# A gated delta-rule scan whose state is updated one leaf earlier, with one carry matmul for keys and queries

## What is computed

```python
def step(St, inp):
    kt, qt, vt, at, bt = inp
    Sk = jnp.einsum('bhij,bhj->bhi', St, kt)
    err = Sk - vt
    Sn = at[..., None] * St - (bt[..., None] * err)[..., None] * kt[:, :, None, :]
    ot = jnp.einsum('bhij,bhj->bhi', Sn, qt)
    return (Sn, ot)
```

## Time and profile before

| | |
|---|---|
| median of 3 runs | 8708.34 us (8691.14 to 8710.81) |
| the profiled execution's time | 8691.16 us |
| its span | 8689.2 us |
| scan phase in it | from about 1112 to 3980 us |
| projection phase in it | from about 194 to 1095 us |
| PE, DVE, ACT, POOL busy, whole span | 74%, 59%, 27%, 32% |

### The profile page before, as it was taken

How to read it: one execution, slowest core, us unless ns; L and a number is a source line. 1 busy time by engine, 2 the same in 40 slices (tenths; PEclk the granted TensorE clock), 3 DMA queues, 4 the chain that set the end, 5 groups by cost and what they waited for, 6 DMA issues and landing times. The chain is left out here.

```text
span 8689.2 us, 99856 instructions
## 1 busy us (share of the span) xinstructions
PE 6422.4 (74%) x25312; PEld 4362.9 (50%) x25312; DVE 5122.4 (59%) x8030; ACT 2321.9 (27%) x4571; POOL 2792.5 (32%) x4069
## 2 busy tenths in 40 slices
PE   2888746666666666667898987745528989898799
PEld 1766635555555555554456863322217832222587
DVE  3888846667676666765564221487887743433322
ACT  1222212222222222223342111244411233333111
POOL 0555557777777777772111111000000000000011
PEclk6999855555555555557998998856555578888899
DMA  4333343334343434332211013211103211111200
GB/s 163 120 136 136 131 103 89 94 82 97 84 97 84 95 82 98 84 84 83 69 47 54 22 51 122 65 29 36 30 1 68 51 39 30 39 29 33 94 29 27
DMA packets 939691, 631.50 MB, mean 73 GB/s; under 512 B 764768, under 2 KB 841056, under 8 KB 906080
## 3 DMA queue, kind: packets, MB, share of 16 engines
q1 hardware_dynamic: 939280, 627.52, 26.3%
HBM read 437.68 MB, written 192.81 MB: 73 GB/s over the span
## 5 line engine op out<-in xcount | busy, mean ns | idle before, releaser
L897 POOL TENSOR_TENSOR ffn_hid_low<-ffn_hid,ffn_hid_high 128x512 fp32r<-128x512 f32 x128 | 164.6, 1286 | 3560.3 <-ACT ffn_hid_high L887 3560.3
L298 PE MATMUL proj_acc<-proj_xn,proj_w 128*128 128x512 f32 x3072 | 732.5, 402 | 121.9 <-ACT proj_decay L344 87.8
L1413 POOL TENSOR_TENSOR scan_ud<-scan_ud,scan_ring 128x16 f32<-128x16 f32 (+6 forms) x1792 | 629.9, 352 | 548.0 <-DVE scan_ud L1516 412.5
L2150 PE MATMUL attend_ot<-attend_e,attend_v 128*64 128x512 f32 (+3 forms) x1280 | 678.0, 619 | 92.4 <-ACT attend_e L2177 92.4
L298 PEld LDWEIGHTS proj_acc<-proj_xn,proj_w 128*128 128x128 f32 x3072 | 598.3, 195 | 256.2 <-ACT proj_decay L344 90.8
L1442 POOL TENSOR_TENSOR scan_pq<-scan_qs,scan_ud 128x320 f32<-128x320 f32 (+3 forms) x512 | 655.8, 1307 | 0.0
L1516 DVE TENSOR_REDUCE scan_ud<-scan_pk 128x16 f32<-128x48 f32 (+6 forms) x1792 | 558.0, 311 | 67.2 <-DVE scan_pk L1513 6.7
L393 DVE SCALAR_TENSOR_TENSOR proj_y<-proj_raw,proj_cw,proj_y 128x2048 f32<-128x2048 f32 x144 | 575.6, 3997 | 19.1 <-DVE proj_y L389 2.9
L1774 PE MATMUL csum_sc<-csum_qk 96*128 96x512 f32 (+3 forms) x640 | 290.3, 570 | 395.6 <-ACT csum_e L1798 350.2
L1288 PE MATMUL scan_krow<-scan_kbd,scan_duT 128*128 128x64 f32 x1536 | 411.7, 432 | 166.5 <-ACT scan_duT L1200 166.5
L1320 PE MATMUL scan_zq<-scan_ring,scan_S 128*128 128x64 f32 x2048 | 453.3, 422 | 102.4 <-DVE scan_S L1562 102.4
(11 more groups left out here) (211 smaller groups left out, 13407.4 us busy)
## 6 DMA issues: line engine op xcount, KB each, us to landing
scan_abar<-decays SPq DMA_DIRECT2D x64, 1024.0 KB, 4.7
scan_kbd<-kbd SPq DMA_DIRECT2D x64, 768.0 KB, 4.4
csum_qk<-qk SPq DMA_DIRECT2D x96, 256.0 KB
cmax_qk<-qk SPq DMA_DIRECT2D x96, 256.0 KB
attend_qk<-qk SPq DMA_DIRECT2D x96, 256.0 KB
proj_beta_rows<-beta SPq DMA_DIRECT2D x16, 1024.0 KB, 8.1
stream_k<-proj_res SPq DMA_DIRECT2D x16, 1024.0 KB, 3.9
stream_beta_k<-proj_resb SPq DMA_DIRECT2D x16, 1024.0 KB, 3.9
```

Of the source, the lines that this page charges most:

```text
L298: mm = pe.matmul(acc[:, (j * TT + t) % 8, :], w[:, u, wh, j, k, :], xn[:, xh, k, t * TOK:(t + 1) * TOK], start=(p == 0 and k == 0), stop=( ...
L1413: pool.tensor_tensor(ud[:, l, t + 1, 1:t + 1, :], ud[:, l, t, 1:t + 1, :], a, ALU.mult).then_inc(dec_step, 1)
L2150: pe.matmul(ot[:, g % 2, lo:TOK], v[:, u, kt, :], e[:, x % RINGS, lo:TOK], start=(kt == 0), stop=(x == last_of[g])).then_inc(summed, 1)
```

## The change

The change has these parts:

- **State one leaf earlier.** The state of the next window now takes in the last leaf of the window before and leaves 0 to 2 of this one (`uw`, `kin` shifted by a leaf). `ds` and its additions to `S` are done during leaf 3, and the next `z` (`project`) follows. Leaf 3 reaches the next window through a fourth carry: a second Gram product per window (keys 8 tokens back, `gback`, `copy_back`) and a larger `kbd`.
- **One carry matmul.** `carry` multiplies a transposed leaf with keys' and queries' columns together (256 columns, result `y` in PSUM). Leaf 0 gets one too. VectorE takes `y` in at the start of each leaf, with two operations more.
- **Summed index innermost** in `pk` and `pq`, so that the sums read neighbouring elements, and the products read `ud` across.
- **Leaf decays as a sixth stream.** `project_phase` multiplies decays within each leaf of 8 tokens (`within`) and stores them; the scan loads them with the ring and drops `ge`. GpSimd's `tables` has 5 operations in place of 12.
- **Ring loads on ScalarE's queue** (`load_ring`), six DMAs in every second window. Gram numbers are made one window ahead, not two.

The core of the diff (shortened):

```diff
-            def carry_k(l, to, src, parity, first, last):
-                t = LEAF * (to - l - 1)
-                for b in range(2):
-                    mm = pe.matmul(krow[:, to % 2, 8 * b:8 * b + 8, 0, :], duT[:, src, :],
-                                   later(l, parity)[:, 0, 8 * b:8 * b + 8, t:t + LEAF], start=first, stop=last)
+            def carry(c, j, parity):
+                table = kbd[:, parity, KBD_AT[j]:KBD_AT[j + 1]].rearrange("p (w h t) -> p w h t", w=2, h=H)
+                t = LEAF * (c - j)
+                return pe.matmul(y, duT[:, TURNED[c] + j, :], table[:, :, :, t:t + LEAF], start=(j == 0), stop=(j == c))
...
+                    wait(pe, uw_copied, 2 * (w + 1))
...
+                    wait(pe, y_added, 4 * w + 4)
+                    wait(pe, yq_copied, 4 * w + 4)
+                    wait(pe, ut_copied, w + 1)
...
+                    wait(pe, qb_copied, 8 * (w + 1))
+                    wait(pe, s_added, 4 * (w + 1))
+                    project(n[0], n[1])
+                    broadcast_k(n[0], 0)
```

```diff
 # ScalarE, start of a window
+                copy_tr(w, 0, 0, 1)
+                copy_yq(w, 0)
+                copy_kin(w, tok)
+                if u == 0 and not first or u == WPC and not final:
+                    wait(act, kin_copied, w + 1)
+                    wait(act, table_step, 5 * (w + 1))
+                    load_ring(act, it if u == 0 else it + 1, 1 - u // WPC)
+                copy_slot(w, tok, 1)
+                if more:
+                    n = at(it, u, 1)
+                    copy_back(n[0])
+                    copy_gram(n[0])
```

```diff
 # VectorE, in a leaf, and the order of a window
+                yk = y[:, 0]
+                dve.tensor_tensor(ud[:, l, 1, 1, :], pk[:, l, 0, :, 0], yk[:, :, 0], ALU.add).then_inc(u_step, 1)
+                later = yk[:, :, 1:LEAF].rearrange("p h t -> p t h")
+                dve.tensor_tensor(later, later, ud[:, l, 1:LEAF, 0, :], ALU.mult).then_inc(y_scaled, 1)
+                wait(dve, y_scaled, 4 * w + l + 1)
+                dve.tensor_tensor(pk[:, l, 1:LEAF, :, 0], pk[:, l, 1:LEAF, :, 0], later, ALU.add).then_inc(y_added, 1)
...
+                    dve.tensor_reduce(ud[:, l, t + 1, t + 1, :], pk[:, l, t, :, 0:t + 1], AX.X, ALU.add).then_inc(u_step, 1)
+                    between(t)
...
+                leaf(w, 0, nothing)
+                if more:
+                    split_gram(at(it, u, 1)[0])
+                prepare_k(w, tok, parity, 1, LEAVES - 1, 2)
+                if not first:
+                    reduce_o(*before, 2)
                 prepare_q(w, parity)
-                leaf(w, 1)
-                leaf(w, 2)
+                leaf(w, 1, nothing)
+                if not first:
+                    reduce_o(*before, 3)
+                leaf(w, 2, nothing)
                 reduce_o(w, it, u, 0)
...
+                def add_state(t):
+                    if more and t >= LEAF - R:
+                        r = t - (LEAF - R)
...
+                leaf(w, 3, add_state)
                 reduce_o(w, it, u, 1)
```

More of the change, by code:

```diff
@@ L1149, in body @@
                         store_o(it - 1, 1)
[L1150 to L1151 removed]
+                if more:
                     load_rows(n[0], 2)
+                    load_rows(n[0], 3)
                     wait(sp, s_decayed, 4 * (w + 1))
                     load_abar(n[0])
[L1155 to L1170 removed]
+            run(sp, prologue, body)
             store_o(TURNS - 1, 1)
@@ L1273, in broadcast_q @@
                 wait(pe, rows_in[l], 64 * (w + 1))
+                first = rows_of(l, 1)
                 for b in range(2):
                     if l == 0:
-                        wait(pe, pre_step, 5 * (w + 1))
+                        wait(pe, pre_step, 6 * (w + 1))
                     else:
                         wait(pe, qb_copied, 8 * w + 2 * (l - 1) + b + 1)
-                    pe.matmul(zq[:, b, :], ones[32:34, :], rows[32:34, l, 512 * b:512 * b + 512],
+                    pe.matmul(zq[:, b, :], ones[first:first + 2, :], rows[first:first + 2, l // 2, 512 * b:512 * b + 512],
@@ L1292, in carry_q, with project @@
-            def carry_q(to, src, parity):
-                for l in range(to):
-                    t = LEAF * (to - l - 1)
-                    mm = pe.matmul(yq, duT[:, src + l, :], later(l, parity)[:, 1, :, t:t + LEAF], start=(l == 0), stop=(l == to - 1))
-                return mm
-            def turn_leaf(w, l, n):
-                wait(pe, u_step, 32 * w + 8 * (l + 1))
-                wait(pe, dec_step, 28 * w + 7 * (l + 1))
-                pe.transpose(tr[:, 0, :], ud[:, l, LEAF, 1:SLOTS, :].rearrange("p s h -> p (s h)"), idt[:, :]).then_inc(tr_done, 1)
-                wait(pe, tr_copied, 5 * w + n + 1)
+            def project(w, tok):
+                for h in range(H):
+                    mm = pe.matmul(z[:, h], S[:, h, :], ring[:, 0:2, h, tok:tok + WIN], start=True, stop=True)
+                mm.then_inc(z_done, 1)
@@ L1354, in body @@
-                wait(pe, yq_copied, 3 * w + 2)
+                wait(pe, y_added, 4 * w + 2)
+                wait(pe, yq_copied, 4 * w + 2)
+                turn_older(w, 2, 3)
+                for j in range(2):
+                    carry(2, j, parity)
+                turn_last(w, 2, 4)
+                carry(2, 2, parity).then_inc(y_done, 1)
+                broadcast_k(w, 3)
+                wait(pe, y_added, 4 * w + 3)
+                wait(pe, yq_copied, 4 * w + 3)
                 wait(pe, kin_copied, w + 1)
```

566 lines of the change are left out of this document (287 added, 279 removed).

## The result

The changed kernel takes 9155.1 us (median of 4 runs, 9148.97 to 9167.66), the kernel before took 8706.08 us beside it. The ratio is 1.0521, with a 95% interval of 1.0502 to 1.0539. The forecast was 9230 us, so its sign and mechanism were right and its size 75 us too high.

What follows compares the result with a forecast made beforehand. A chain of waits, not a full engine, was taken to bound the kernel. 8691 + 185 (longer windows) + 355 (ring loads) + 5 (prologue) = 9236 us, given as 9230; own range 9130 to 9350, wider 8940 to 9360.

Steps and rivals of the forecast that it cites:

- the last step of the sum: From 9236 us, against the profiled execution, to the forecast median of 9230; the median before was 17 us above that execution.
- Ring loads, +355: Six DMA issues on ScalarE ahead of the Gram copies delay leaf 1 by 11.8 us in 30 windows: +355 us.
- Rival 1: Ring DMA issues on ScalarE are short, 0.39 us each: +70 us in all, 8951 us; chance 17%.
- L0 to L1: Gap from leaf 0's start to leaf 1's, filled by VectorE's work: 9.3 us against 8.2, without the ring issues.
- L1 to L2: Gap from leaf 1 to leaf 2: later copies and wider carries make VectorE wait; 8.3 us against 6.6.
- L2 to L3: Gap from leaf 2 to leaf 3: broadcasts, transposes and three carries precede the last carry; 10.6 us against 8.3.
- Rival 2: The queue's additions hide: L1 to L2, L2 to L3 stay 6.6, 8.3; 8981 us (8%), or 8696 with short issues (3%).
- L3 to L0: Gap from leaf 3 to the next leaf 0, shortened by the earlier state update: 18.9 us against 21.1.
- z and the turn stand in one queue: On TensorE leaf 3's turn (0.84 us) stands behind z (7.08) and a key broadcast (0.75), losing most of the gain.
- faster sums don't help here: From leaf 1 to leaf 2 VectorE waits some 2 us anyway; output sums save 0.26 and 0.43 us each.
- Rival 3: TensorE's clock rises to 2.4 GHz: window 37.4 us, 8620 us in all; decides from 38.5 us a window; chance 5%.
- Rival 4: The tables come late under the ring's traffic, 5 us in each of 30 windows: 9390 us; chance 6%.

Runs made afterwards that it cites:

- ring_spread: Changed kernel with the six ring DMAs issued apart on ScalarE's queue: one, one, then four at the window's end; 8820.6 us, 1.0154 of the kernel before.
- turn_carry: Changed kernel with z in four groups, each behind its quarter of S, leaf 3's transpose before the last group and its carry right behind z; 8822.2 us.
- older_first: Changed kernel with the older leaves' transposes and carries ahead of the queries' second broadcasts on TensorE, ScalarE's copies in the same order; 9041.1 us.
- Quarters: Changed kernel with z's matmuls in four groups, each waiting only for its own quarter of the addition to S; 8896.9 us.
- sum_outer: Changed kernel with only the layout of the outputs' products put back, so that their sums read across memory again; 9194.4 us.
- all_spread: Changed kernel with the edits of ring_spread, turn_carry and older_first together; 8478.3 us, 0.9766 of the kernel before.
- all_early: all_spread with ring DMAs issued earlier, four of the six before the window's end; 8390.6 us, 0.9644 of the kernel before.
- ring_late: Changed kernel with all six ring DMAs issued on ScalarE after the window's last copy; 8864.8 us, 1.0182 of the kernel before.

## Why the prediction was right, point by point

- **Sign and mechanism.** Both added terms are where they were put: the window by itself, and the issues on ScalarE. By the sums of gaps, undoing only the place of the issues (ring_spread, -338 us) gives back the one; turn_carry (-316) and older_first (-111) more than give back the other. The total is nearer than its working by luck in one place, the last step of the sum, and further off by a term that the forecast had at nothing, the clock (both below).
- **Ring loads, +355:** measured +344, 11.5 us in 30 windows. Rival 1 has fallen: the waits are there, and a ring load is issued in 0.38 us only when none stands right ahead of it.
- **L0 to L1, L1 to L2, L2 to L3:** 9.3, 8.3 and 10.6 forecast, 9.03, 8.20 and 10.87 measured. VectorE's waits ahead of leaves 2, 3 and 0 were given as 2, 4.6 and 1.5 us and are 2.41, 3.85 and 2.22 in the window shown (means 2.4, 4.25 and 2.4). That the broadcasts ahead of the carries set L2 to L3 is shown by older_first. For L1 to L2 it explains 0.59 of 1.46 us; the rest (later `y`, carries of 256 columns) was argued, and no run took it apart. Rival 2 has fallen. The third gap is nearer to its forecast than its steps are: where the clock stays at 1.2 GHz it is 11.22 us, not 10.87.
- **L3 to L0, the term that was mis-sized:** 18.9 forecast, 17.60 measured; 1.3 us in 63 windows are 82 us, about the size of the whole error. The step was "the update matmuls end at 4.1 [...] four additions and three steps end at 9.0": the last addition ends at 2481.86, 7.7 us after leaf 3 (2474.18), and at 7.1 us in the window ahead of it, where the first addition starts 3.0 us after leaf 3. So the update was ready a good microsecond earlier than forecast in most windows, and additions and steps together took 4.1 us in place of 4.8. From the last addition to leaf 0 the forecast had 9.9 us; it is 10.4 (2481.86 to 2492.22). The early update is the clock's doing. In six of the 63 windows the clock stays at 0.50 from leaf 2 to the next leaf 0, and they come close to the forecast; one of them (window view, then VectorE), and last the first 3.0 us of the leaf 3 at 2428.86, whose clock is at 1.00:

```profile
2635.53:2653.86 18.33, 12.67 (x74) 10.40 (x73) 8.21 (x26) 1.35 (x4) 7.84 (x15) 0.50 0.17 59
...
2635.53 0.18 DVE L1550 TENSOR_TENSOR scan_ud<-scan_pk,scan_misc 128x16 f32<-128x16 f32 x1 [4.62 <-PE scan_misc L1329]
...
2639.45 0.69 DVE L1615 TENSOR_TENSOR scan_S<-scan_S,scan_misc 128x512 f32<-128x512 f32 x1 [1.28 <-PE scan_krow L1418]
...
2428.86:2431.86 3.00, 1.48 (x35) 1.07 (x33) 2.32 (x11) 1.07 (x3) 1.41 (x6) 1.00 0.10 6
```

The update is ready 3.9 us after leaf 3 there (4.1 forecast) and 3.0 where the clock is up; leaf 3 to leaf 0 is 18.3 us against 17.4, and leaf 2 to leaf 3 is 11.22 with VectorE's wait at the forecast 4.6. At 1.2 GHz throughout, the two gaps would thus be some 46 and 22 us longer over the scan (an estimate from 18.33 and 11.22 against the means).

- **The sum's last step** is wrong: 9236 us stood against the profiled execution, and with the 17 us up to the median it gives 9253, not 9230. Against 9253 the miss is 98 us, and the profiled execution (9148.97 us) is 87 below 9236; by the estimate above some 68 of these are the clock's.
- **"z and the turn stand in one queue":** shown. Quarters gave 4.06 us, the turn and carry 1.06 more.
- **Sums:** "faster sums don't help here" is shown by sum_outer. Taken at 1.7 ns per element, the product across was right: 339 ns against 0.15 + 112 x 0.0017 = 0.34 us.
- **Rival 3, the clock:** the kernel did not get faster, and the granted clock is 0.55 over the scan. But the clock does rise for a part of 57 of 63 windows, around leaf 3, which the forecast had at nothing; that is the mechanism of rival 3 in small. Its 38.5 us a window is the length at which the scan would make up for the loads ((38.5 - 44.2) x 63 = -359), and says nothing of when the clock rises.
- **Rival 4, late tables:** not seen. In windows with and without a load the median gaps from leaf 1 on are 8.20 and 8.20, 11.22 and 10.64, 17.41 and 17.41 us. The difference in the second pair goes with the clock: 11.2 to 11.4 us wherever it stays at 0.50 up to leaf 3, with a load or without.
- **Prologue and projection, +5 and 0:** the first leaf starts 1.2 us later than before, so both together cost about nothing; they were not measured apart.

## What to carry over

Removing work from a chain pays only as far as the in-order queues around it let it: here a detour got shorter by a leaf's length, and z behind four additions instead of two, two broadcasts ahead of the carries and six DMA issues ahead of a small copy cost more than that. Before moving a step, write down for each engine what stands behind it and who waits for that; the same arithmetic in another order went from 5.2% slower to 3.6% faster. The next wait can come from an engine that none of the edits touched, as GpSimd's did in leaf 3. Issue DMAs singly, into stretches where the issuing engine idles, and early enough to land.

## What the runs showed of the hardware

**The clock moves within a window.** In the kernel before it was 0.50 throughout the scan. In the changed one it is 0.87 in the stretch after leaf 3 starts, and 0.50 again at the end of the update matmuls:

```profile
2474.18:2477.00 2.82, 1.41 (x28) 1.20 (x30) 2.33 (x11) 1.07 (x3) 1.18 (x5) 0.87 0.45 99
...
2476.50:2477.00 0.50, 0.50 (x17) 0.50 (x16) 0.29 (x2) 0.00 (x0) 0.28 (x2) 0.50 0.70 279
```

Before the rise TensorE was busy 9.21 of 10.69 us with broadcasts and three wide carries; in the stretch at the high clock it was busy half of the time. The fall comes before the 4.2 us in which TensorE idles ahead of z. The clock has risen by the last carry into leaf 3 (0.70 us at 2473.35, in place of 1.22) and the transposes of `uw` behind it (0.60, where the keys' four take 1.06 in the earlier trace rows); this is why the update was ready early. In all_spread, three stretches behind leaf 3:

```profile
2534.44:2538.00 3.56, 2.12 (x37) 1.36 (x35) 1.61 (x8) 2.04 (x5) 3.13 (x5) 1.00 0.08 5
2538.00:2539.67 1.67, 0.00 (x0) 0.03 (x1) 1.52 (x6) 0.00 (x0) 1.02 (x3) 1.00 0.25 35
2541.00:2544.00 3.00, 3.00 (x16) 3.00 (x16) 2.96 (x7) 0.00 (x0) 2.48 (x6) 0.50 0.53 221
```

The clock is at 2.4 GHz while TensorE idles for 2.3 us ahead of z, and falls to 1.2 GHz when z, which starts at 2539.67 and runs without a pause, is about a microsecond old. So in both kernels the fall comes while TensorE is busy, and the work just before it is sparser than before the rise. Not every window shows a rise. One of all_early, which is as short as any here:

```profile
2461.92:2501.76 39.84, 34.25 (x182) 22.82 (x182) 26.88 (x87) 12.35 (x31) 30.27 (x51) 0.50 0.29 78
```

TensorE is busy 86% of it, and the clock stays at 1.2 GHz. What tells such a window from the others, and where the clock rises for good, was not found.

**An issue's length varies with other queues.** Six issues on ScalarE gave 2.30 us each from the fourth on in the changed kernel, but one each of 5.48 us (ring_late) and 5.67 us (ring_spread) at the window's end. In both cases SyncE had issued the load of `abar` 1 to 3 us before; ring_spread has:

```profile
2484.08 0.38 SPq L1114 DMA_DIRECT2D scan_abar<-decays  x1
```

That this load is the cause was not tested.
